# Second-layer linear attention: query products of the second half moved ahead of the key transposes, and the transposes put through four PSUM banks in two rounds

## The chip, the cores and the metric

The kernel runs on one core of one Trainium2 chip. The metric is the time of one execution on the device in microseconds; the time before is 3043.68 us, the median of three runs (3041.82 to 3044.96).

## The reference, cut to what matters

Four images of 64x64 tokens with 128 channels pass through two layers. The first is softmax attention over all 4096 tokens of an image, and takes most of the time. The second has a linear attention, and a routed mixture of experts behind it. The change is in the linear attention:

```python
def _L1_attn_ref(x, W_qkv, W_out, b_out, gn_w, gn_b):
    ...
    qkv = jnp.einsum('oc,bcl->bol', W_qkv, xc)
    q, k, v = jnp.split(qkv, 3, axis=1)
    ...
    q = jax.nn.softmax(q, axis=2) * scale      # over the 32 channels of a head
    k = jax.nn.softmax(k, axis=3)              # over all tokens of an image
    context = jnp.einsum('bhcj,bhdj->bhcd', k, v)
    out = jnp.einsum('bhcd,bhdi->bhci', context, q)
    out = out.reshape(b, h * d, l)
    out = jnp.einsum('oc,bcl->bol', W_out, out) + b_out[None, :, None]
    ...
```

The softmax of the keys runs over all tokens, so the context (a 128x128 matrix) can be summed only once every key chunk has been exponentiated, and no output token exists before the context does.

## The kernel before

The program is written engine by engine, each with its own instruction stream; semaphores tie them together, and each engine works strictly in the order of its stream. The outer loop runs over the four images (batches). Within one, the first layer's attention comes first (512 key tiles of 128 by query chunks of 512), and then the stretch that the change is in, about 75 us of each batch.

In that stretch the 4096 tokens are eight chunks of 512 (`NCH` = 8, `HCH` = 4, `CH` = 512, `TPB` = 4 tiles of 128 a chunk). PSUM has eight banks `BK[0]` to `BK[7]`, one chunk of 512 columns each. Chunk c uses bank c for everything: its transposed input, then its keys (channels by tokens), then its values (tokens by channels), then its queries. Each bank must be read out before TensorE writes it again.

TensorE (`pe`): for each half (chunks 0 to 3, then 4 to 7) it transposes the normed input, makes the keys, then the values. For the first half it makes the queries as well. Then it turns the exponentiated keys K over, chunk by chunk in the order `k_order` = 4, 5, 6, 7, 0, 1, 2, 3, each into its own bank (L1356 to L1364); then makes the queries of chunks 4 to 7 (L1365 to L1367); then sums the context over 32 tiles (L1369 to L1372, into `BK[0]`), which waits for the last copy of the transposed keys. Then the queries, exponentiated and normalised, are turned in the order `q_order` = 1 to 7, 0, and the output products follow.

ScalarE (`act`): copies the first half's values, exponentiates query chunks 0 and 1, exponentiates the keys in two pieces of 2048 columns (L610), copies the second half's values (`values1`, L588), exponentiates query chunks 2 and 3 (L602), copies the eight chunks of transposed keys to `KT` (L617), exponentiates query chunks 4 to 7, and later copies the transposed queries (L621).

VectorE (`dve`): takes each query chunk's maximum over each head (L962), subtracts it and writes `QE` (L963, `q_shifted`), and sums the exponentials and takes the reciprocal (L970, L971, `q_summed`). L988 scales the context to `CTX`, and L993 makes the output weights `AT`. The sums of chunks 5, 6, 7 and 0 stand behind L988 in its stream. GpSimd multiplies `QE` by the reciprocals (L484), chunk by chunk behind L971.

Semaphores at the change: `s_v1c` counts value chunks copied out by ScalarE, `s_q1` query products done, `s_q1s` query chunks read out of PSUM by L963, `s_q1e` query chunks exponentiated, `s_k1e` key exponentials, `s_kT` transposed key chunks in PSUM, `s_kTc` transposed key chunks copied to SBUF.

All matrix work in the trace goes through two helpers: L1134 is any product, L1139 any transpose. A 128x128 product is two MATMUL records, a transpose one.

Of the kernel before, what the change touches and what calls it, by code (L numbers as in the profile page):

```python
# [25 lines left out]
ACT = mybir.ActivationFunctionType  # L26
X_AX = mybir.AxisListType.X

P = 128
B = 4  # L30
N = 64 * 64
C = 128
# [3 lines left out]
CH = 512  # L36
NCH = N // CH
# [74 lines left out]
HCH = NCH // 2  # L112
# [10 lines left out]
def hybrid_kernel(nc, x, w_qkv0, w_out0, b_out0, w_qkvT, w_outT, b_out1, gn_w, gn_b, router_w, router_b,  # L123
# [5 lines left out]
    with ctx:  # L129
        def sb(name, shape, dt=F32, stack=ctx):  # L130
            return stack.enter_context(nc.sbuf_tensor(name, shape, dt))

        def sem(name):
            return ctx.enter_context(nc.semaphore(name))
# [9 lines left out]
        K = sb("K", [P, N])  # L144
# [7 lines left out]
        KT, QE, Z = KE[:, 0:N], KE[:, N:2 * N], KE[:, 2 * N:3 * N]  # L152
# [16 lines left out]
        WQKV1 = sb("WQKV1", [P, 3 * C])  # L169
# [53 lines left out]
        BK = [BK8[:, i, :] for i in range(8)]  # L223
# [60 lines left out]
        s_v1c = sem("s_v1c")  # L284
        s_q1 = sem("s_q1")
        s_q1s = sem("s_q1s")
# [3 lines left out]
        s_kT = sem("s_kT")  # L290
        s_kTc = sem("s_kTc")
# [211 lines left out]
        def _(act):  # L503
            act.sem_inc(s_pvc, 1)
            for b in range(batches):
# [93 lines left out]
                def q_exponentials(chunks):  # L599
                    for c in chunks:  # L600
                        act.wait_ge(s_q1s, b * NCH + c + 1)
                        nc.scalar.activation(QE[:, c * CH:(c + 1) * CH], QE[:, c * CH:(c + 1) * CH],  # L602
                                             ACT.Exp).then_inc(s_q1e, 1)
# [10 lines left out]
                q_exponentials(range(HCH // 2, HCH))  # L614
                for i, c in enumerate(k_order):
                    act.wait_ge(s_kT, b * NCH + i + 1)
                    nc.scalar.activation(KT[:, c * CH:(c + 1) * CH], BK[c], ACT.Copy).then_inc(s_kTc, 1)  # L617
                q_exponentials(range(HCH, NCH))
                for i, c in enumerate(q_order):
                    act.wait_ge(s_qT, b * NCH + i + 1)  # L620
                    nc.scalar.activation(QT[:, c * CH:(c + 1) * CH], BK[c], ACT.Copy).then_inc(s_qTc, 1)  # L621
# [30 lines left out]
        def _(dve):  # L652
# [101 lines left out]
            for b in range(batches):  # L754
# [201 lines left out]
                def q_shifted(chunks):  # L956
                    for c in chunks:
                        g = slice(c * TPB * H, (c + 1) * TPB * H)
                        dve.wait_ge(s_q1, b * NCH + c + 1)
                        q = BK[c].rearrange("p (g d) -> p g d", d=D)  # L960
                        e = QE[:, c * CH:(c + 1) * CH].rearrange("p (g d) -> p g d", d=D)
                        mix_link(v.reduce_max(QM[:, g], q, X_AX))  # L962
                        v.tensor_tensor(e, q, QM[:, g].unsqueeze(2).to_broadcast([P, TPB * H, D]),  # L963
                                        ALU.subtract).then_inc(s_q1s, 1)

                def q_summed(places):
                    for c in q_order[places]:
                        g = slice(c * TPB * H, (c + 1) * TPB * H)
                        dve.wait_ge(s_q1e, b * NCH + c + 1)
                        mix_link(v.reduce_sum(QSUM[:, g], QE[:, c * CH:(c + 1) * CH].rearrange("p (g d) -> p g d", d=D), X_AX))  # L970
                        v.reciprocal(QSUM[:, g], QSUM[:, g]).then_inc(s_q1r, 1)  # L971
# [5 lines left out]
                mix_link(v.reduce_max(SMALL[:, 10:11], MXS[:, :], X_AX))  # L977
                v.tensor_scalar(SMALL[:, 8:9], SMALL[:, 10:11], -1.0, None, ALU.mult).then_inc(s_k1x, 1)
                q_shifted(range(HCH // 2, HCH))
                q_summed(slice(0, HCH - 1))  # L980
                q_shifted(range(HCH, NCH))
                q_summed(slice(HCH - 1, HCH))

                dve.wait_ge(s_k1e, b * 2 + 2)
                mix_link(v.tensor_tensor(SMALL[:, 9:10], KSUM[:, 0:1], KSUM[:, 1:2], ALU.add))
# [146 lines left out]
        def _(pe):  # L1132
            def mm(o, lhsT, rhs, start=True, stop=True, shared=False):
                return nc.tensor.matmul(o, lhsT, rhs, start=start, stop=stop, skip_group_check=shared)  # L1134

            def transposes(dst, src, c):

                for t in range(c * TPB, (c + 1) * TPB):
                    last = nc.tensor.transpose(dst[:, (t % TPB) * P:(t % TPB + 1) * P], src(t), IDENT)  # L1139
                return last  # L1140
# [21 lines left out]
            for b in range(batches):  # L1162
# [169 lines left out]
                def token_major(c, weights, signal):  # L1332
                    for t in range(c * TPB, (c + 1) * TPB):
                        last = mm(BK[c][:, (t % TPB) * C:(t % TPB + 1) * C], XT[:, t * P:(t + 1) * P], weights)
                    last.then_inc(signal, 1)

                for half in range(2):
# [13 lines left out]
                    if half == 0:  # L1351
                        for c in chunks:
                            pe.wait_ge(s_v1c, b * NCH + c + 1)
                            token_major(c, WQKV1[:, 0:C], s_q1)

                for i, c in enumerate(k_order):  # L1356
                    if i % HCH == 0:
                        pe.wait_ge(s_k1e, b * 2 + i // HCH + 1)

                    if c >= HCH:  # L1360
                        pe.wait_ge(s_v1c, b * NCH + c + 1)
                    else:
                        pe.wait_ge(s_q1s, b * NCH + c + 1)
                    transposes(BK[c], lambda t: K[:, t * P:(t + 1) * P], c).then_inc(s_kT, 1)  # L1364
                for c in range(HCH, NCH):  # L1365
                    pe.wait_ge(s_kTc, b * NCH + c - HCH + 1)
                    token_major(c, WQKV1[:, 0:C], s_q1)  # L1367

                pe.wait_ge(s_kTc, b * NCH + NCH)  # L1369
                for t in range(T):  # L1370
# [137 lines left out]
```

## Time and profile before

| | |
|---|---|
| median of three runs | 3043.68 us |
| those runs | 3041.82, 3044.96, 3043.68 us |
| profiled execution, its own time | 3042.56 us |
| its span in the trace | 3040.7 us |
| mean granted TensorE clock | 0.981 of full |
| busy: TensorE, VectorE, ScalarE, GpSimd | 2873.7, 2574.7, 2411.2, 711.9 us |

The span is the time from the first instruction to the last of the profiled execution; 1.9 us of its own time lie around it. In the views, PE is TensorE, PEld its weight loads, DVE VectorE, ACT ScalarE, POOL GpSimd. "L1134" is a line of the kernel.

### The profile page before, as it was taken

The page shows a single profiled execution, that of the slowest core. Times are in us where ns is not written, and L with a number is a line of the kernel's source. Part 1 is how long each engine was busy: PE and PEld are TensorE (multiplying, and loading weights), DVE is VectorE, ACT ScalarE, POOL GpSimd, SP SyncE. Part 2 cuts the span into 40 slices and gives each one's busy share as a digit, 9 for nine tenths or more (in the row PEclk, how much of TensorE's full clock was granted, in tenths as well). Part 3 has the DMA queues.
Part 4 walks back from the last instruction along what each step waited for, and adds up shares of the span by engine and source line. Part 5 has one row for each costly group of instructions (what it writes and reads, how often), then busy time and mean ns, then how long its engine had stood idle before and what let it go on. Part 6 is the DMA issues. An engine that isn't in the chain of part 4 may idle for free.

```text
span 3040.7 us, 52573 instructions
## 1 busy us (share of the span) xinstructions
PE 2873.7 (95%) x20414; PEld 1005.8 (33%) x20414; DVE 2574.7 (85%) x3687; ACT 2411.2 (79%) x3141; POOL 711.9 (23%) x726
## 2 busy tenths in 40 slices
PE   6999999989899999998889999999898999999988
PEld 3222222275422222227532222223743222222474
DVE  5888889878888888887888888898788888888877
ACT  4999999843799999975479999997448999999634
POOL 1122222113412222211432222121153222122115
PEclk9999999998999999999999999999999999999999
DMA  2655565500165555550026555554003555555400
GB/s 86 117 112 106 109 114 113 104 1 14 56 119 107 111 113 109 111 98 1 15 72 117 112 111 111 106 104 92 1 21 61 110 111 112 102 108 109 77 1 28
DMA packets 72081, 257.03 MB, mean 85 GB/s; under 512 B 8160, under 2 KB 10240, under 8 KB 71808
## 3 DMA queue, kind: packets, MB, share of 16 engines
q0 software_dynamic: 64512, 234.91, 40.9%
q1 hardware_dynamic: 7296, 18.51, 1.6%
q8 instruction: 168, 2.75, 0.4%
q14 instruction: 105, 0.86, 0.1%
HBM read 10.12 MB, written 8.39 MB: 6 GB/s over the span
## 4 chain that ended last, share of the span: by engine, by line
PE 84%; DVE 8%; ACT 5%; issue 2%; POOL 1%; SPq 0%; DMA 0%; POOLq 0%; DVEq 0%; ACTq 0%
PE BK L1134 82%; ACT EA L559 2%; DVE X L1103 2%; ACT KE L559 2%; PE BK L1139 2%; DVE MXS L953 1%; DVE ST L679 1%; ACT K L610 1%; POOL KE L484 1%; ACT SMC L548 0%; DVE KE L711 0%; DVE RU L673 0%; DVE RU L672 0%; DVE XT L836 0%; DMA XN<-in_x 0%
## 5 line engine op out<-in xcount | busy, mean ns | idle before, releaser
L889 DVE TENSOR_TENSOR XT<-XT,KE 128x512 f32<-128x512 f32 x1344 | 1573.0, 1227 | 148.9 <-ACT KE L559 146.5
L559 ACT ACTIVATE KE<-BK 128x512 f32<-128x512 f32 (+1 forms) x1536 | 1490.6, 1023 | 129.9 <-PE BK L1134 34.1
L1134 PE MATMUL BK<-Q,K 32*128 32x512 f32 x8192 | 1167.9, 640 | 18.5 <-ACT KE L559 12.2
L1134 PE MATMUL BK<-KE,V 128*32 128x512 f32 x6144 | 815.1, 604 | 5.3 <-ACT SMC L548 5.3
L443 POOL DMA_DIRECT2D RM<-EA x448 | 392.8, 957 | 1506.9 <-ACT EA L559 650.6
L1134 PEld LDWEIGHTS BK<-Q,K 32*128 32x128 f32 x8192 | 320.0, 183 | 874.7 <-ACT KE L559 626.6
L559 ACT ACTIVATE EA<-BK 128x512 f32<-128x512 f32 (+1 forms) x512 | 497.5, 1026 | 26.5
L1134 PEld LDWEIGHTS BK<-KE,V 128*32 128x32 f32 x6144 | 125.4, 108 | 582.7 <-issue 533.0
L1134 PE MATMUL BK<-EA,V 128*32 128x512 f32 x2048 | 272.7, 604 | 0.0
L1134 PE MATMUL BK<-WEXP,XT 128*128 128x512 f32 x512 | 246.0, 628 | 13.9 <-DVE X L1103 13.9
L647 ACT ACTIVATE RM<-BK,GT 128x128 f32<-128x128 f32 x512 | 145.5, 368 | 137.3 <-PE BK L1134 137.3
L1103 DVE SCALAR_TENSOR_TENSOR X<-BK,GT,X 128x128 f32<-128x128 f32 x512 | 175.4, 350 | 33.4 <-PE BK L1134 17.3
L863 DVE TENSOR_TENSOR XT<-KE 128x512 f32<-128x512 f32 x64 | 88.7, 1390 | 124.4 <-ACT KE L559 124.4
L493 POOL TENSOR_TENSOR Z<-RM 128x512 f32<-128x512 f32 x64 | 81.1, 1268 | 266.7 <-ACT RM L647 266.7
L1134 PEld LDWEIGHTS BK<-WEXP,XT 128*128 128x128 f32 x512 | 99.0, 203 | 126.4 <-issue 94.8
L424 POOL TENSOR_TENSOR Q<-PVC,REC 128x512 f32<-128x512 f32 x32 | 70.1, 2192 | 251.0 <-DMA RM<-EA 120.5
L1134 PEld LDWEIGHTS BK<-EA,V 128*32 128x32 f32 x2048 | 40.7, 108 | 193.5 <-issue 171.1
L843 DVE RECIPROCAL REC<-SMC 128x512 f32<-128x512 f32 x28 | 93.7, 3345 | 0.0
L1134 PE MATMUL BK<-WQKV,XT 128*128 128x128 f32 x768 | 89.4, 276 | 0.0
L1134 PEld LDWEIGHTS BK<-WQKV,XT 128*128 128x128 f32 x768 | 87.9, 192 | 4.0 <-issue 3.8
L1134 PE MATMUL BK<-XT,WQKV 128*128 128x512 f32 x192 | 88.1, 613 | 0.5 <-ACT XT L510 0.5
L836 DVE TENSOR_TENSOR XT<-XT,RM 128x512 f32<-128x512 f32 x64 | 75.3, 1217 | 0.0
(182 smaller groups left out, 1803.1 us busy)
## 6 DMA issues: line engine op xcount, KB each, us to landing
RM<-EA POOLq DMA_DIRECT2D x224, 768.0 KB, 6.7
RM<-EA POOLq DMA_DIRECT2D x224, 256.0 KB, 3.3
XN<-in_x SPq DMA_DIRECT2D x16, 512.0 KB, 6.1
out<-X SPq DMA_DIRECT2D x16, 512.0 KB, 2.6
WEXP<-in_L_ffn_expert_w SPq DMA_DIRECT2D x1, 512.0 KB, 6.8
CONST<-in_consts SPq DMA_DIRECT2D x1, 384.0 KB, 5.7
WQKV<-in_L_conv_w_qkv SPq DMA_DIRECT2D x1, 192.0 KB, 2.3
WQKV<-in_L_attn_W_qkv SPq DMA_DIRECT2D x1, 192.0 KB, 5.9
```

Source lines behind the costliest of these rows:

```text
L424: nc.gpsimd.tensor_tensor(Q[:, c * CH:(c + 1) * CH], PVC[:, :], REC[:, :], ALU.mult).then_inc(s_ot, 1)
L443: nc.gpsimd.dma_start(DACC[:, PART[p]], EA[:, k % 2, PART[p]], accum_op=ALU.add).then_inc(s_dacc[p], 16)
L493: nc.gpsimd.tensor_tensor(Z2[:, :, :], z[:, :, 0:2 * C], z[:, :, 2 * C:4 * C], ALU.add).then_inc(s_zs, 1)
L559: nc.scalar.activation(exps(jt, p), scored(c * T + jt, p).rearrange("p a n -> p (a n)"), ACT.Exp, scale=SCALE0).then_inc(s_exp, 1)
L647: last = nc.scalar.activation(ZX[:, t // 2 % 2, t % 2, k], expert_bank(t, 1)[:, k], ACT.Copy, scale=GT[:, t, e:e + 1])
L836: v.tensor_tensor(acc, acc, DACC[:, PART[p]], ALU.add).then_inc(s_merge, 1)
L843: v.reciprocal(REC[:, :], row_sums).then_inc(s_rec, 1)
L863: v.tensor_tensor(ACC[:, par, PART[p]], exps(0, p), exps(2, p), ALU.add).then_inc(s_adds, 1)
L889: v.tensor_tensor(acc, acc, exps(jt, p), ALU.add).then_inc(s_adds, 1)
L1103: v.scalar_tensor_tensor(X[:, t, :], expert_bank(t, 0)[:, e * C:(e + 1) * C], GT[:, t, e:e + 1], X[:, t, :], ALU.mult, ALU.add).then_inc(s ...
L1134: return nc.tensor.matmul(o, lhsT, rhs, start=start, stop=stop, skip_group_check=shared)
L1139: last = nc.tensor.transpose(dst[:, (t % TPB) * P:(t % TPB + 1) * P], src(t), IDENT)
```

## The change

TensorE makes the second half's queries before any key transpose. The transposes then take banks 0 to 3 only, the place in the order taken modulo four: the first four (chunks 4 to 7) wait until VectorE has read the first half's queries from those banks, the last four (chunks 0 to 3) until ScalarE has copied out the transposed chunk that was put there one round earlier. ScalarE's four query exponentials of the second half, which came behind the eight copies, are put between them, one behind every second copy. VectorE sums one query chunk instead of three before it takes the second half's queries, and three instead of one behind them. No instruction is added or left out.

```diff
@@ ScalarE
                 for i, c in enumerate(k_order):
                     act.wait_ge(s_kT, b * NCH + i + 1)
-                    nc.scalar.activation(KT[:, c * CH:(c + 1) * CH], BK[c], ACT.Copy).then_inc(s_kTc, 1)
-                q_exponentials(range(HCH, NCH))
+                    nc.scalar.activation(KT[:, c * CH:(c + 1) * CH], BK[i % HCH], ACT.Copy).then_inc(s_kTc, 1)
+                    if i % 2:
+                        q_exponentials([HCH + i // 2])
@@ VectorE
                 q_shifted(range(HCH // 2, HCH))
-                q_summed(slice(0, HCH - 1))
+                q_summed(slice(0, 1))
                 q_shifted(range(HCH, NCH))
-                q_summed(slice(HCH - 1, HCH))
+                q_summed(slice(1, HCH))
@@ TensorE
+                for c in range(HCH, NCH):
+                    pe.wait_ge(s_v1c, b * NCH + c + 1)
+                    token_major(c, WQKV1[:, 0:C], s_q1)
                 for i, c in enumerate(k_order):
                     if i % HCH == 0:
                         pe.wait_ge(s_k1e, b * 2 + i // HCH + 1)
 
-                    if c >= HCH:
-                        pe.wait_ge(s_v1c, b * NCH + c + 1)
+                    if i < HCH:
+                        pe.wait_ge(s_q1s, b * NCH + i + 1)
                     else:
-                        pe.wait_ge(s_q1s, b * NCH + c + 1)
-                    transposes(BK[c], lambda t: K[:, t * P:(t + 1) * P], c).then_inc(s_kT, 1)
-                for c in range(HCH, NCH):
-                    pe.wait_ge(s_kTc, b * NCH + c - HCH + 1)
-                    token_major(c, WQKV1[:, 0:C], s_q1)
+                        pe.wait_ge(s_kTc, b * NCH + i - HCH + 1)
+                    transposes(BK[i % HCH], lambda t: K[:, t * P:(t + 1) * P], c).then_inc(s_kT, 1)
```

## Rows read from the trace of the kernel before

**Rows 1.** The page: busy time by engine, and the chain's shares.
```profile
PE 2873.7 (95%) x20414; PEld 1005.8 (33%) x20414; DVE 2574.7 (85%) x3687; ACT 2411.2 (79%) x3141; POOL 711.9 (23%) x726
...
PE 84%; DVE 8%; ACT 5%; issue 2%; POOL 1%; SPq 0%; DMA 0%; POOLq 0%; DVEq 0%; ACTq 0%
```

**Rows 2.** Windows, batches 1 and 2: length, busy PE, PEld, DVE, ACT, POOL, clock, DMA.
```profile
610.00:800.00 190.00, 168.48 (x830) 118.22 (x829) 150.24 (x450) 91.63 (x239) 53.12 (x57) 0.91 0.03 12
1361.00:1551.00 190.00, 166.41 (x850) 114.89 (x851) 153.06 (x460) 91.42 (x241) 53.14 (x57) 0.94 0.03 12
```

**Rows 3.** The chain that ended last, fourth batch: start us, us, what.
```profile
2899.38 0.49 ACT V L588
...
2915.99 0.35 DVE CTX L988
...
2917.30 4.08 POOL KE L484 x4
...
2922.14 7.16 PE BK L1134 x64
```

**Rows 4.** TensorE's timeline there: start us, us, line, operation, [idle before, releaser].
```profile
2892.73 3.73 PE L1134 MATMUL BK<-WQKV,XT 128*128 128x128 f32 x32
2900.00 5.15 PE L1139 MATMUL BK<-CONST,K 128*128 128x128 f32 x32 [3.54 <-ACT V L588]
2904.99 3.74 PE L1134 MATMUL BK<-WQKV,XT 128*128 128x128 f32 x32
2908.56 7.31 PE L1134 MATMUL BK<-V,KE 128*128 128x128 f32 x64
2915.71 1.91 PE L1139 MATMUL BK<-CONST,KE 128*128 128x128 f32 x16
```

**Rows 5.** ScalarE's timeline there.
```profile
2899.28 2.03 ACT L588 ACTIVATE V<-BK 128x512 f32<-128x512 f32 x4
2901.19 1.16 ACT L602 ACTIVATE KE<-KE 128x512 f32<-128x512 f32 x2
2902.23 4.01 ACT L617 ACTIVATE KE<-BK 128x512 f32<-128x512 f32 x8
...
2902.23 0.60 ACT L617 ACTIVATE KE<-BK 128x512 f32<-128x512 f32 x1
...
2916.35 2.07 ACT L621 ACTIVATE EA<-BK 128x512 f32<-128x512 f32 x4 [4.21 <-PE BK L1139]
```

**Rows 6.** VectorE's timeline there.
```profile
2897.83 0.67 DVE L970 TENSOR_REDUCE QSUM<-KE 128x16 f32<-128x512 f32 x1
2898.53 0.25 DVE L971 RECIPROCAL QSUM<-QSUM 128x16 f32<-128x16 f32 x1
...
2906.09 0.69 DVE L962 TENSOR_REDUCE QM<-BK 128x16 f32<-128x512 f32 x1 [2.41 <-PE BK L1134]
...
2907.42 0.68 DVE L962 TENSOR_REDUCE QM<-BK 128x16 f32<-128x512 f32 x1
```

**Rows 7.** Short windows, columns as in rows 2.
```profile
644.40:650.00 5.60, 5.55 (x26) 5.58 (x27) 1.74 (x4) 5.10 (x11) 2.05 (x2) 0.50 0.01 3
...
2900.00:2903.00 3.00, 3.00 (x14) 3.00 (x15) 1.10 (x3) 3.00 (x7) 0.08 (x1) 0.50 0.00 0
2903.10:2904.90 1.80, 1.80 (x19) 1.80 (x18) 0.54 (x2) 1.80 (x5) 1.80 (x2) 1.00 0.00 0
...
1493.20:1496.60 3.40, 3.40 (x8) 1.84 (x9) 2.31 (x5) 0.00 (x0) 0.00 (x0) 0.52 0.00 0
...
677.50:680.80 3.30, 3.30 (x6) 1.75 (x7) 2.26 (x14) 0.00 (x0) 0.00 (x0) 0.51 0.01 2
```

**Rows 8.** TensorE's timeline at three other pauses, batches 1 and 2.
```profile
1493.14 1.00 PE L1436 MATMUL BK<-CONST,G 128*128 128x128 f32 x4 [2.63 <-DVE GT L1084]
```
```profile
1476.62 1.98 PE L1134 MATMUL BK<-WEXP,XT 128*128 128x512 f32 x4 [1.59 <-DVE X L1103]
```
```profile
676.40 0.38 PE L1134 MATMUL BK<-MV,CONST 128*128 128x1 f32 x2 [1.31 <-DVE MV L1002]
```

## The prediction, as it was made before the result was known

> **What bounds the kernel now.** The page says that TensorE is busy 95% of the span and carries 84% of the chain that ended last [rows 1], but that is an average in which the first layer weighs most. The change touches only the second layer's linear attention, so I read the chain of waits there, in the fourth batch [rows 3]. The reader is to see that no engine has slack in it. ScalarE's first value copy, on the chain from 2899.38 behind the key exponentials, frees a bank, TensorE starts at 2900.00 and works without a pause through the key transposes (32 records), the query products (32) and the context (64), until 2915.87 [rows 4]; then VectorE scales the context, GpSimd normalises four query chunks and TensorE makes the output. Whatever moves the start of the context moves the end of the batch by the same amount, unless something behind it was waiting for another engine. The other batches have the same chain with the same pieces, so each cost counts four times.
>
> TensorE's timeline [rows 4] gives the four numbers to hold on to: a pause of 3.54 us up to 2900.00, the queries' products from 2904.99, the context from 2908.56, its end at 2915.87. ScalarE's timeline [rows 5] shows why that context starts without a wait: the eight copies of transposed keys run from 2902.23 to 2906.24, while TensorE transposes and then makes queries. The last copy ends 2.3 us before the context needs it. **The query products are what hides the copies.** The change takes that cover away.
>
> **What starts TensorE.** Before, the first transpose waits for the copy of the values in bank 4 (s_v1c). After, the first query product waits for the same copy, since queries of chunk 4 go to bank 4. So TensorE starts again at 2900.0, and the pause of 3.54 us stays. Banks 0 to 3 would have been free earlier, but the transposes that use them stand behind the products. Gain at the start: nothing, from either side; only a reordering of the stream could give one.
>
> **TensorE's 64 records.** The stretch from 2900.0 begins at half clock (1.2 GHz, granted 0.50) and is at full clock (2.4 GHz) from about 2903.0 [rows 7]. At full clock 32 product records run in 3.57 us (2904.99 to 2908.56 [rows 4]), 0.112 us each, and the 16 transposes of rows 4 in (1.91 - 0.28)/15 = 0.109 us each. Product and transpose records cost the same, so it does not matter which of them fall into the slow 3 us: 32 transposes now take 4.99 us there (2900.00 to 2904.99), and 32 products will too. Products end at 2905.0, transposes follow. Sum so far: 0.
>
> **VectorE.** A chunk has 8 product records: 1.8 us at half clock for chunk 4. VectorE starts a chunk 1.10 us after its product starts at full clock (2904.99 to 2906.09 [rows 4, 6]), so 0.2 us after its records; chunk 4 can be taken from 2902.0. Each chunk costs 1.33 us (2906.09 to 2907.42 [rows 6]), so the shifted queries are there at about 2903.4, 2904.7, 2906.0 and 2907.4. Only one sum (L970 and L971, some 0.9 us from 2897.83 [rows 6]) stands ahead of them now. Then three sums of some 0.9 us, to 2910.1, all before the context's scaling. The sums of chunks 5, 6, 7 and 0 still stand behind L988, so the tail from the context to the output (rows 3: 2915.99 to 2922.14, with GpSimd's 4.08 us) is not shortened. Gain: 0.
>
> **ScalarE, and the term that decides.** Spacing of copies: (4.01 - 0.60)/7 = 0.487 us, where 0.60 is one copy [rows 5]. Spacing of exponentials: 2901.19 to 2902.23 for two, 0.52 each [rows 5]. A transposed chunk is 4 records, 0.44 us, and ScalarE starts 0.64 us after its first record (2915.71 to 2916.35 [rows 4, 5]). So:
>
> - the first transpose starts at 2905.05, the first copy at 2905.69;
> - transposes come every 0.44 us and copies every 0.487, so from there ScalarE has a queue and never waits;
> - before the eighth copy it does seven copies and three exponentials: 7 x 0.487 + 3 x 0.52 = 4.97 us, and the exponentials' inputs (2903.4 to 2906.0) are always there in time. The eighth copy starts at 2910.66 and ends at 2911.26;
> - TensorE follows 0.13 us behind a copy's end (2899.38 + 0.49, transpose at 2900.00 [rows 3, 4]). The context starts at 2911.39 instead of 2908.56: **2.83 us later**.
>
> TensorE itself hardly waits for banks: its fifth transpose is ready at 2906.8, the first copy done at 2906.3; the seventh waits about 0.2 us, the eighth 0.3. It has turned the last chunk by 2909.1, and then stands idle for some 2.3 us. That is where the loss shows. Four batches: 4 x 2.83 = 11.3 us. The fourth exponential falls behind the last copy and costs nothing.
>
> Bounds of this term. If the exponentials cost nothing between the copies, 4.97 shrinks to 3.41, and the context starts 1.27 us late: 5.1 us in all. If every step of ScalarE took its full 0.60 us instead of overlapping the next, ten steps would be 6.0 us and the delay 3.86: 15.4 us in all. I take the measured spacings, since copies and exponentials already stand next to each other without a gap: values to 2901.19, two exponentials, then copies from 2902.23 [rows 5].
>
> **The clock.** The new pause is on TensorE's path, and the clock may fall behind it. Rows: the pause of 2.63 us ahead of L1436 is followed by 3.4 us at half clock (granted 0.52), in all four batches alike; a pause of 1.59 us by none; one of 1.31 us with a small product and 0.7 us more, 2 us in all, by half clock in the first batch only, 3.3 us at 0.51 [rows 7, 8]. Mine is 2.3 us plus two short waits, nearer to 2.63. A stretch of 3.4 us at half clock costs 1.7 us, some of it spent in the pause itself; 1.5 us then. I take three batches of four: 4.5 us. Bounds: nothing, and 4 x 1.7 = 6.8 us. Beside this, shifting the later batches changes where other slow stretches fall: batch 1 now has a mean of 0.91 over 190 us, batch 2 0.94 [rows 2], which is 0.03 x 190 = 5.7 us of full clock between two batches with the same work. That can go either way, and widens the range on both sides, more upward, because three of the four batches show the better figure now (0.94, 0.94, and the fourth the same stretches).
>
> By the Trainium skill, page "TensorE: Matmul & The Clock Gate", section "Part 4: PE-mode transpose", transposes do not count as activity for the clock, so that products placed first should bring it back sooner. In this trace the clock came back at 2903.0 behind 3 us of transposes alone, so I give this no term; by the rule, 3 us at half clock would shrink at most to 0 and return 1.5 us a batch.
>
> **Sum.** Own time of the profiled execution 3042.56 + 11.3 + 4.5 = 3058.4 us; against the median, 3043.68, that execution is 1.1 us short. I forecast 3058.4 us.
>
> **Rivals.**
>
> A. ScalarE's queue as above, but the clock stays up in the new pause, or nearly: 3042.56 + 11.3 = 3053.9. For it: 1.59 us left the clock alone. Against it: 2.63 us never did. Chance 0.20.
>
> B. Only latency: the copies keep pace with the transposes because the exponentials cost almost nothing there, and only the last copy is bare: 3042.56 + 5.1 = 3047.7, with at most a clock fall or two. Against it stands 0.52 us each. Chance 0.08, part of it within 0.2% (6.1 us), which is about what a measurement of this kernel can tell from no change.
>
> C. The other side, not slower: the clock. Its place is the start at 2900.0 and the slow stretches behind it. In the first batch the half clock lasts from before 644.4 to beyond 650.0, 26 records, where the others have 3 us from the restart [rows 7]. If products first, or the shifted phase, brought the clock back earlier, a batch would win up to 1.5 us at 2900 (2.8 in the first) and up to 5.7 us over the rest of the first batch. It decides only from 11.3 us on, that is, 22.6 us less at half clock in all; 1.5 x 3 + 2.8 + 5.7 = 13.0 would do it, if all of it came and the new pause cost nothing. Chance 0.03. The Trainium skill, in the section on transposes named above ("TensorE: Matmul & The Clock Gate", Part 4), would speak for the first part of it, 1.5 us a batch.
>
> D. No effect: the products would have to go on hiding the copies, or the tail have slack of 2.8 us. GpSimd's and VectorE's pieces behind the context are bare in the chain, so I see none. Chance 0.03.
>
> E. Worse: all four pauses drop the clock, and the shifted batches pick up more slow stretches: 3053.9 + 6.8 = 3060.7, and up to 5.7 more, 3066.4. Chance 0.16.
>
> My forecast (queue and two to four falls of the clock, 3056 to 3061) has 0.50. To hold eight in ten the range runs from 3051 to 3065: it leaves out B, C, D and the end of E. Faster by over 0.2%: 0.02; within 0.2% (up to 3049.8): 0.07; slower: 0.91.
>
> **What the profile of the changed kernel would show.** The start of the query products, 3.5 us behind the values, as before: right for the first step. The last key transpose some 2 us ahead of the context, with the context's idle put down to ScalarE's L617: right for the queue. Spacing of 0.49 and 0.52 us on ScalarE from the first copy to the eighth: right for its price; gaps there would mean that VectorE or TensorE sets the pace. The distance from the context's end to the output's start unchanged at 6.3 us. Granted clock 0.5 behind the pause in most batches. I am wrong if the context starts less than 1.5 us later than before relative to the first value copy, or if the tail behind it shortens.

## The result, and the profile after

The changed kernel takes 3057.32 us (median of five runs, 3055.97 to 3059.27), against 3043.04 us for the kernel before (five runs). The ratio is 1.0047, 95% interval 1.0036 to 1.0057: slower by 14.3 us, between 11 and 17. The prediction was 3058.4 us, range 3051 to 3065. The profiled execution took 3055.97 us, span 3054.2 us, 13.5 us more span than before.

In the changed kernel lines behind 979 stand one further down: products are L1135, transposes L1140, the scaling of the context L989. First the chain that ended last in the fourth batch (start us, us, what), to be laid beside [rows 3]:

```profile
2910.64 5.18 PE BK L1135 x32
2915.82 0.45 PE BK L1140 x4
...
2916.29 1.09 ACT KE L617 x2
2917.38 0.52 ACT KE L602
2917.90 0.97 ACT KE L617 x2
2918.87 0.52 ACT KE L602
2919.39 0.97 ACT KE L617 x2
2920.36 0.52 ACT KE L602
2920.88 0.98 ACT KE L617 x2
...
2921.91 7.43 PE BK L1135 x64
...
2929.43 0.35 DVE CTX L989
```

Before, the chain stayed on TensorE from 2900.00 to the context's end:

```profile
2900.00 5.15 PE BK L1139 x32
2905.15 10.73 PE BK L1134 x96
```

Now it leaves TensorE behind the first transposed chunk, runs over eleven steps of ScalarE (eight copies, three exponentials), and comes back only for the context. TensorE's timeline of the same stretch, beside [rows 4]:

```profile
2910.64 5.18 PE L1135 MATMUL BK<-WQKV,XT 128*128 128x128 f32 x32 [3.44 <-ACT V L588]
2915.66 3.92 PE L1140 MATMUL BK<-CONST,K 128*128 128x128 f32 x32
2921.91 7.41 PE L1135 MATMUL BK<-V,KE 128*128 128x128 f32 x64 [2.32 <-ACT KE L617]
```

In this batch the restart is as before (a pause of 3.44 us, then 32 records in 5.0 us), the transposes follow, and ahead of the context stands a new pause of 2.32 us, released by the copy. All four batches have it, at 2.32 or 2.33 us.

The distances, taken from TensorE's timelines (start of the first record of each kind, us). "Restart" is the first record behind the pause of 3.5 us, "output" the first output product, "the next attention" the next batch's first product of queries and keys:

| batch | restart to context, before | after | context to output, before | after | output to the next attention, before | after |
|---|---|---|---|---|---|---|
| first | 9.91 | 12.77 | 13.42 | 15.15 | 143.52 | 141.60 |
| second | 8.44 | 11.51 | 13.42 | 13.52 | 141.60 | 141.59 |
| third | 8.53 | 11.55 | 13.42 | 13.51 | 141.62 | 142.98 |
| fourth | 8.56 | 11.27 | 13.42 | 13.52 | 118.72 (to the end) | 118.77 |

The context is late by 2.86, 3.07, 3.02 and 2.71 us, 11.7 in all. From there to the output only the first batch differs much: 1.73 us. The rest of the batch gives 1.9 back in the first and takes 1.4 more in the third. Sum: 11.7 + 2.0 - 0.5 = 13.2, and some 0.3 us ahead of the restarts make the 13.5 of the spans.

The 11.7 us have two parts, by the same timelines. From the first key transpose to the context it is 6.25 us in every batch, where it was 3.57 from the first query product to the context: 2.68 us a batch, 10.7 in all. The other 0.95 us lie in the 32 records behind the restart. As query products they take 6.52, 5.26, 5.30 and 5.02 us, where the 32 transposes before took 6.33, 4.87, 4.96 and 4.99.

The clock behind the new pause, in windows (length, busy PE, PEld, DVE, ACT, POOL, then the granted clock), first and second batch:

```profile
657.20:661.00 3.80, 3.77 (x19) 3.77 (x20) 0.00 (x0) 0.49 (x1) 0.00 (x0) 0.55 0.00 0
...
1413.00:1416.00 3.00, 3.00 (x27) 3.00 (x28) 0.00 (x0) 0.42 (x1) 0.19 (x1) 1.00 0.00 0
```

The reader is to see the same pause and two outcomes: half clock behind it in the first batch, full clock in the second. The third and fourth are like the second.

### The profile page after: what moved, and what is told of

The parts are those of the page before. It is cut to its first block, busy times and chain, and to the rows that moved or that the text cites. A ratio compares the mean times of both kernels' runs of the same rounds, so it can differ in the third digit from the quotient of the medians.

```text
span 3054.2 us, 52573 instructions
## 1 busy us (share of the span) xinstructions
PE 2881.0 (94%) x20414; PEld 1014.4 (33%) x20414; DVE 2576.3 (84%) x3687; ACT 2410.4 (79%) x3141; POOL 710.9 (23%) x726
## 4 chain that ended last, share of the span: by engine, by line
PE 83%; DVE 8%; ACT 6%; issue 2%; POOL 1%; DMA 0%; SPq 0%; POOLq 0%; DVEq 0%; ACTq 0%
PE BK L1135 82%; ACT EA L559 2%; DVE X L1104 2%; ACT KE L559 2%; PE BK L1140 1%; DVE MXS L954 1%; DVE ST L680 1%; ACT K L610 1%; POOL KE L484 1%; ACT KE L617 1%; ACT SMC L548 0%; DVE KE L712 0%; DVE RU L674 0%; DVE RU L673 0%; DVE XT L837 0%
## 5 line engine op out<-in xcount | busy, mean ns | idle before, releaser
L1135 PE MATMUL BK<-Q,K 32*128 32x512 f32 x8192 | 1167.8, 640 | 18.5 <-ACT KE L559 12.2
L1135 PE MATMUL BK<-KE,V 128*32 128x512 f32 x6144 | 815.0, 604 | 5.3 <-ACT SMC L548 5.3
L1135 PEld LDWEIGHTS BK<-Q,K 32*128 32x128 f32 x8192 | 319.9, 182 | 874.8 <-ACT KE L559 626.6
L1135 PEld LDWEIGHTS BK<-KE,V 128*32 128x32 f32 x6144 | 125.3, 108 | 582.7 <-issue 533.0
L1135 PE MATMUL BK<-EA,V 128*32 128x512 f32 x2048 | 272.6, 604 | 0.0
L1135 PE MATMUL BK<-WEXP,XT 128*128 128x512 f32 x512 | 239.1, 613 | 13.9 <-DVE X L1104 13.9
L1135 PEld LDWEIGHTS BK<-WEXP,XT 128*128 128x128 f32 x512 | 95.6, 196 | 122.3 <-issue 90.3
L1135 PE MATMUL BK<-WQKV,XT 128*128 128x128 f32 x768 | 97.2, 290 | 13.8 <-ACT V L588 13.8
L1135 PEld LDWEIGHTS BK<-EA,V 128*32 128x32 f32 x2048 | 40.7, 108 | 193.5 <-issue 171.1
L1135 PEld LDWEIGHTS BK<-WQKV,XT 128*128 128x128 f32 x768 | 95.3, 205 | 18.5 <-ACT V L588 14.5
L1135 PE MATMUL BK<-XT,WQKV 128*128 128x512 f32 x192 | 89.0, 618 | 0.5 <-ACT XT L510 0.5
```

## The experiments

Each was timed against the kernel before on the same chip. A figure such as "+14" is us over it. None of the kernels leaves work out; the added transposes of four of them (e4, e5, e8, e9) write into a bank that is overwritten before anything reads it. A row with fewer than 64 records of V,KE is cut off by the end of the view, not by the kernel.

### e1: the exponentials back behind the copies

```diff
                     nc.scalar.activation(KT[:, c * CH:(c + 1) * CH], BK[i % HCH], ACT.Copy).then_inc(s_kTc, 1)
-                    if i % 2:
-                        q_exponentials([HCH + i // 2])
+                q_exponentials(range(HCH, NCH))
```

> The changed kernel with ScalarE's four exponentials of the second half put back behind the eight copies; TensorE and VectorE as changed. Theory (ScalarE's queue decides when the context starts): before the eighth copy there are seven copies and no exponential, 3.41 instead of 4.97 us, so from the first query product to the context it is about 9.8 us in a batch, against 8.5 before and 11.3 to 11.6 in the changed kernel; the time is some 5 us over before, with the clock up to 8. Rival (the loss comes from the clock, or from products ahead of transposes as such): the distance stays at 11 us or more and the time at 13 to 14 us over before.

Measured: 3043.03 us against 3043.37, ratio 0.9998 (0.9989 to 1.0007). The mechanism came as worked out and the total did not. TensorE's timeline, second batch:

```profile
1398.48 5.44 PE L1134 MATMUL BK<-WQKV,XT 128*128 128x128 f32 x32 [3.44 <-ACT V L588]
1403.76 3.66 PE L1139 MATMUL BK<-CONST,K 128*128 128x128 f32 x32
1408.48 3.73 PE L1134 MATMUL BK<-V,KE 128*128 128x128 f32 x31 [1.06 <-ACT KE L617]
```

The pause has shrunk from 2.33 to 1.06 us, and restart to context is 10.00 us (fourth batch 9.93): 1.5 us less than in the changed kernel in the second batch, and 1.4 to 1.6 more than before. From the first key transpose to the context it is 4.72 us in every batch, where it was 6.25: the three exponentials cost 1.53 us in the queue, and 1.56 were worked out for them. Yet those 1.4 us, four times, are nowhere in the total. They are won back behind the output in all four batches: output to the next attention takes 140.14 and 140.17 us in the second and third batch, where it took 141.60 and 141.62. My theory of the queue stands; that delays simply add up does not. e8 asks why. e1 also divides the loss: the products moved ahead of the transposes, with the four banks, cost nothing in the total, and the 14 us come only with the exponentials put between the copies. The exponentials there, with the products left behind the transposes, were not run.

### e2: the sums in their old order

```diff
                 q_shifted(range(HCH // 2, HCH))
-                q_summed(slice(0, 1))
+                q_summed(slice(0, HCH - 1))
                 q_shifted(range(HCH, NCH))
-                q_summed(slice(1, HCH))
+                q_summed(slice(HCH - 1, HCH))
```

> The changed kernel with VectorE's sums in their old order (three chunks ahead of the second half's queries, one behind). Theory: VectorE takes chunk 4's queries about 1.5 us later, and they are still there before ScalarE asks for them behind its second copy; nothing moves, 14 us over before as the changed kernel. Rival (VectorE's order is what holds ScalarE): ScalarE waits at its exponentials and the time rises by a further 2 us or more.

Measured: 3057.68 us, ratio 1.0044 (1.0028 to 1.0059), +14, as the changed kernel. Restart to context is 11.55 us in the second batch (after: 11.51), and ScalarE's steps stand as close as before. VectorE's new order does nothing.

### e3: the four banks alone

TensorE, ScalarE and VectorE in their old orders, and only the banks of the transposes changed, with the waits that this asks for (ScalarE's copy, not shown, reads the same bank):

```diff
                 for i, c in enumerate(k_order):
                     if i % HCH == 0:
                         pe.wait_ge(s_k1e, b * 2 + i // HCH + 1)
-                    if c >= HCH:
-                        pe.wait_ge(s_v1c, b * NCH + c + 1)
+                    if i < HCH:
+                        pe.wait_ge(s_q1s, b * NCH + i + 1)
                     else:
-                        pe.wait_ge(s_q1s, b * NCH + c + 1)
-                    transposes(BK[c], lambda t: K[:, t * P:(t + 1) * P], c).then_inc(s_kT, 1)
+                        pe.wait_ge(s_kTc, b * NCH + i - HCH + 1)
+                    transposes(BK[i % HCH], lambda t: K[:, t * P:(t + 1) * P], c).then_inc(s_kT, 1)
                 for c in range(HCH, NCH):
-                    pe.wait_ge(s_kTc, b * NCH + c - HCH + 1)
+                    pe.wait_ge(s_v1c, b * NCH + c + 1)
                     token_major(c, WQKV1[:, 0:C], s_q1)
```

> The old order on TensorE (transposes, then products of the second half) and old orders on ScalarE and VectorE, but the transposes through four banks in two rounds. Theory (what was lost is the cover of the products over the copies): the first round runs inside the old pause, some 2 us earlier, the second waits for the copies and ends at about the time at which it ended before; products cover the last copies again, so the context starts within 0.5 us of before and the time is within 3 us of before. Rival (the two rounds in four banks cost in themselves): 5 us or more over before.

Measured: 3041.58 us against 3043.37, ratio 0.9992 (0.9983 to 1.0001). No loss.

```profile
1394.37 1.97 PE L1139 MATMUL BK<-CONST,K 128*128 128x128 f32 x16 [0.99 <-ACT K L610]
1399.91 3.41 PE L1139 MATMUL BK<-CONST,K 128*128 128x128 f32 x16 [3.57 <-ACT KE L617]
1403.11 3.97 PE L1134 MATMUL BK<-WQKV,XT 128*128 128x128 f32 x32
1406.92 3.29 PE L1134 MATMUL BK<-V,KE 128*128 128x128 f32 x28
```

The first round runs in what was the pause, because banks 0 to 3 are free early; the second waits 3.57 us for ScalarE's first key copy, and then runs at half clock (3.41 us for 16 records that took 1.97 in the first round). The products cover the last copies, as I expected: the context follows them without a wait. But it does not start within 0.5 us of before. Counted from the start of the key exponentials on ScalarE (1392.22 here), it is 14.70 us, where it was 13.14 before in that batch (1393.69 to 1406.83): 1.6 us late, and in the first batch 0.1. So e3 is a second kernel, after e1, that is late by some 1.5 us in most batches and not slower. Its output to the next attention is 140.2 us in the second batch, like e1's. What it settles is that the two rounds in four banks do not cost time in themselves.

### e4: the old pause filled

```diff
+                pe.wait_ge(s_q1s, b * NCH + 1)
+                for _ in range(7):
+                    transposes(BK[0], lambda t: XT[:, t * P:(t + 1) * P], 0)
                 for i, c in enumerate(k_order):
```

> The kernel before, with 28 extra transposes into bank 0 in TensorE's 3.5 us pause ahead of the key transposes; what they write is overwritten. It prices the clock alone. Theory: the clock stays at full behind the pause, and the distance from the first key transpose to the context falls from 8.5 us (9.9 in the first batch) to 7.1; 1.4 us in three batches and 2.8 in the first, so 7 us less than before. Rival (transposes do not keep the clock up, or the clock is set by something else): no difference, or a later restart, 0 to 2 us more.

Measured: 3039.89 us, ratio 0.9987 (0.9978 to 0.9996), -3.5.

```profile
1392.40 3.22 PE L1139 MATMUL BK<-CONST,XT 128*128 128x128 f32 x28
1396.11 3.77 PE L1139 MATMUL BK<-CONST,K 128*128 128x128 f32 x32 [0.48 <-ACT V L588]
1399.71 3.74 PE L1134 MATMUL BK<-WQKV,XT 128*128 128x128 f32 x32
1403.29 1.95 PE L1134 MATMUL BK<-V,KE 128*128 128x128 f32 x16
```

Restart to context is 7.18 us in every batch: 1.3 to 1.4 less in three, 2.7 in the first, 6.7 in all, as expected. The transposes in the pause hold the clock up. But about half of it is lost later: output to the next attention takes 142.0 us in the first batch and 143.7 and 142.1 in the next two, where it took 143.5, 141.6 and 141.6, and in the fourth it is 120.7 us from the output to the end, where it was 118.7. That is 3.0 us back, net.

### e5: the new pause filled

```diff
+                pe.wait_ge(s_q1s, b * NCH + HCH + 1)
+                for _ in range(5):
+                    transposes(BK[4], lambda t: K[:, t * P:(t + 1) * P], 0)
                 pe.wait_ge(s_kTc, b * NCH + NCH)
```

> The changed kernel with 20 extra transposes into bank 4 behind the key transposes, in the new pause of 2.3 us; what they write is overwritten. Theory (the pause costs its length, through ScalarE's queue, and only now and then the clock): the context starts as late as in the changed kernel; the clock falls behind it in no batch, which is worth 1.6 us where it fell (one batch in the profile of the changed kernel); the time is 12 to 14 us over before. Rival (most of the loss is the clock's): the time comes back to 5 to 8 us over before.

Measured: 3053.85 us against 3042.51, ratio 1.0037 (1.0024 to 1.0049), +11.3, just below what I had written. In the first batch the context starts 12.69 us behind the restart, as late as after (12.77), but the output follows 13.52 us later instead of 15.15. That is the 1.6 us of the clock; the other batches are nearly unchanged from restart to output (11.36 and 11.46 us to the context in the second and third). The new pause costs its length. Its clock costs some 3 of the 14 us by the medians (the two intervals overlap), and 1.6 in the profiles from restart to output.

### e8 and e9: the kernel before, with a delay alone

```diff
                 pe.wait_ge(s_kTc, b * NCH + NCH)
+                for _ in range(3):      # six in e9
+                    transposes(BK[1], lambda t: XT[:, t * P:(t + 1) * P], 0)
```

> The kernel before, with 12 extra transposes into bank 1 between the last key copy and the context, in every batch; what they write is overwritten. At full clock they take 12 x 0.11 = 1.3 us, so the context starts about as late as with the exponentials put back behind the copies (1.4 us a batch later than before), and that kernel was not slower than before. Theory (a delay of this size moves the slow stretches of TensorE's clock behind it, and what the batch loses ahead of the output it wins back there): within 2 us of before. Rival (delays simply add up, and that kernel won its time in another way): 5 us over before.

> The same with 24 extra transposes, 2.6 us, so the context starts nearly as late as in the changed kernel (2.7 to 3.1 us a batch later than before), with no other part of the change. Theory (the changed kernel's loss is the late context, four times, and what the clock makes of it): 10 to 14 us over before. Rival (the change costs in another place as well): at most 8 us over before.

Measured: e8 3044.50 us against 3042.79, ratio 1.0005 (0.9996 to 1.0014), +1.7. e9 3054.49 us, ratio 1.0042 (1.0028 to 1.0055), +11.7. In the second batch the context is 9.88 and 11.22 us behind the restart: 1.4 and 2.8 late. 1.4 us in each batch cost next to nothing in all, 2.5 to 2.8 us cost 11.7. Here is where e8 wins back, in windows of the second batch: the routing products and transposes, and the pause ahead of the second gates (before, then e8, then after):

```profile
1443.80:1470.00 26.20, 23.75 (x119) 17.61 (x118) 21.31 (x81) 6.74 (x22) 2.71 (x3) 0.80 0.00 1
1490.00:1500.00 10.00, 7.37 (x17) 3.44 (x16) 7.98 (x22) 3.25 (x12) 3.32 (x5) 0.83 0.00 0
```
```profile
1445.60:1471.30 25.70, 23.75 (x119) 17.64 (x118) 21.04 (x81) 6.69 (x21) 2.72 (x3) 0.80 0.00 1
1491.30:1501.30 10.00, 7.37 (x27) 3.72 (x26) 8.69 (x24) 4.16 (x15) 4.84 (x6) 1.00 0.01 2
```
```profile
1450.00:1476.20 26.20, 24.91 (x109) 19.46 (x108) 19.80 (x77) 6.09 (x18) 1.99 (x2) 0.67 0.00 1
1496.20:1506.20 10.00, 7.37 (x24) 3.50 (x23) 8.69 (x25) 4.03 (x16) 4.15 (x5) 1.00 0.00 0
```

Each has the same pause of 2.63 us ahead of the gates' transposes [rows 8]. In the kernel before the clock falls behind it (0.83 over 10 us, 17 matmul records in it); in e8 it does not (1.00, 27 records), and neither does it in the changed kernel, which pays in the routing stretch instead (0.67 where the others have 0.80, and 109 records in 26.2 us where before has 119: the window is as long, but the work in it is less). Over the same work, from the first routing product (WR) to the first run of twelve expert products (WEXP), it is 25.9 us before, 25.7 in e8 and 27.6 after; from the gates' transposes to the next attention 68.7, 67.0 and 67.0. Over output to the next attention, e8 takes 140.17 us in the second batch, before and after 141.6. So a delay ahead decides which of several slow stretches fall where. e8 confirms that a pure delay of 1.4 us is compensated for the greater part, without any other part of e1. Why the clock falls behind one pause of 2.63 us and not behind another is not settled by these runs.

The timelines of all kernels, laid side by side, show more than e8 alone. This is the length of a batch, from the start of one context to the start of the next (us; e6 and e7 are described below):

| kernels | second context to third | third to fourth |
|---|---|---|
| before, e1, e3, e8 | 750.83, 750.98, 751.05, 750.91 | 750.90, 750.95, 750.99, 751.12 |
| e4 | 751.53 | 750.57 |
| after, e2, e5, e9 | 754.25, 754.30, 754.23, 754.54 | 754.71, 754.71, 754.24, 754.04 |
| e6 | 747.70 | 747.61 |
| e7 | 744.05 | 744.23 |

The lengths lie in four groups with nothing between them. Contexts that are 1.2 to 1.6 us late leave the batch within 0.3 us of its length before; contexts that are 2.5 to 3.1 us late make it longer by 3.1 to 3.8 us, more than the delay. Each kernel was profiled once, and the interval from the first context to the second does not fall into the same groups (752.47 us before, 755.72 after), but the medians of all executions lie in the same order. Why the lengths come in groups is open.

It bears on e9, too. Its profile is 12.0 us longer than that of the kernel before, as much as four late contexts (10.7 us), but not by four equal parts: 2.3 us stand already ahead of the first restart (646.77 us, before 644.45), where the two kernels are the same; the first late context (12.49 us behind the restart, before 9.91) is won back in the rest of its batch; and the later ones cost more than their lateness. That four delays of some 2.7 us and a loss of 11.7 us agree so nearly is in part chance.

### e6: the first round in the old pause, products between

```diff
+                for i in range(HCH):
+                    key_turned(i)
+                second_query(HCH)
+                second_query(HCH + 1)
+                for i in range(HCH, NCH):
+                    key_turned(i)
+                second_query(HCH + 2)
+                second_query(HCH + 3)
@@ ScalarE, in place of values1, q_exponentials and the loop of copies
+                values1(HCH)
+                values1(HCH + 1)
+                for i in range(HCH):
+                    key_copied(i)
+                values1(HCH + 2)
+                values1(HCH + 3)
+                for i in range(HCH, NCH):
+                    key_copied(i)
+                q_exponentials(range(HCH // 2, NCH))
```

`key_turned`, `second_query` and `key_copied` are the bodies of the loops of the changed kernel, with its waits.

> The first round of key transposes stands first and runs inside the old pause (banks 0 to 3 are free 2 us before bank 4 is); then query products of chunks 4 and 5, the second round, products of chunks 6 and 7, the context. ScalarE copies values 4 and 5, keys of round one, values 6 and 7, keys of round two, and exponentiates query chunks 2 to 7 behind them. Theory: ScalarE's twelve copies from 2899.3 take 12 x 0.48 = 5.8 us, so the last one ends at 2905.2, and TensorE's 48 records left take 5.3 us from 2900.4 at full clock; the context starts at 2905.7 to 2907 instead of 2908.56, 1.5 to 2.8 us earlier a batch, 6 to 11 us less than before. Rival (the start of the context isn't set by copies and cover but by TensorE's records and clock alone): within 2 us of before.

Measured: 3025.91 us against 3042.51, ratio 0.9946 (0.9933 to 0.9960), -16.6, more than expected.

```profile
2883.24 1.97 PE L1146 MATMUL BK<-CONST,K 128*128 128x128 f32 x16 [0.99 <-ACT K L610]
2885.71 2.05 PE L1141 MATMUL BK<-WQKV,XT 128*128 128x128 f32 x16 [0.50 <-ACT V L588]
2887.60 1.91 PE L1146 MATMUL BK<-CONST,K 128*128 128x128 f32 x16
2889.34 1.95 PE L1141 MATMUL BK<-WQKV,XT 128*128 128x128 f32 x16
2891.13 7.35 PE L1141 MATMUL BK<-V,KE 128*128 128x128 f32 x64
```

The pause of 3.54 us has become one of 0.99 and one of 0.50, the clock stays up, and the context starts 10.0 us behind the key exponentials' start (2881.09) where it was 13.3 before (2895.30 to 2908.56) and 15.9 after (2906.02 to 2921.91). That is 3.1 to 3.2 us in the last three batches and 4.6 in the first (14.61 before, 10.04 here), 14.1 in all, where 6 to 11 was expected. The upper estimate of 2.8 us a batch already had the 48 records at full clock (5.3 us; they take 5.42); its miss of 0.4 us is mostly the restart, 4.62 us behind the key exponentials' start, where I had counted 5.1. What it left out is the first batch, whose slow stretch was longer: 1.4 us more. The remaining 2.5 us are not assigned; the batches from the second context on are 3.1 and 3.3 us shorter than before (the table above).

### e7: e6, and all sums ahead of the context's scaling

```diff
-                q_summed(slice(1, HCH))
+                q_summed(slice(1, NCH))
                 dve.wait_ge(s_k1e, b * 2 + 2)
                 ...
-                q_summed(slice(HCH, NCH))
                 dve.wait_ge(s_ctx, b * 2 + 2)
```

> As the kernel with the first round in the pause, and VectorE's last four sums ahead of the context's scaling, so that GpSimd normalises while the context is summed. Theory (the tail from the context to the output is set by GpSimd's 4.08 us behind those sums): exponentials end at 2908.3, sums at about 2912, GpSimd at about 2914, near the context's end; the tail shrinks from 6.3 us to about 4, another 2 us a batch, 14 to 19 us less than before in all. Rival (VectorE's sums end behind the context and only change places): no gain over the kernel without it.

Measured: 3015.45 us against 3042.51, ratio 0.9904 (0.9889 to 0.9920), -27 us, where 14 to 19 less was expected. It beats both kernels. It gains 10.5 us over e6, where some 8 were expected; the rest of the surplus is e6's own. GpSimd's timeline, then TensorE's, fourth batch:

```profile
2889.48 7.09 POOL L484 TENSOR_TENSOR KE<-KE,QSUM 128x512 f32<-128x512 f32 x7 [8.42 <-DVE QSUM L978]
```
```profile
2886.47 7.34 PE L1140 MATMUL BK<-V,KE 128*128 128x128 f32 x64
2893.65 1.91 PE L1145 MATMUL BK<-CONST,KE 128*128 128x128 f32 x16
2895.40 0.39 PE L1140 MATMUL BK<-WOUT,CTX 128*128 128x128 f32 x2
2895.62 1.91 PE L1145 MATMUL BK<-CONST,KE 128*128 128x128 f32 x16
2897.37 7.31 PE L1140 MATMUL BK<-AT,EA 128*128 128x128 f32 x64
```

GpSimd works while the context is summed, and the second four query transposes no longer wait for it. Context to output is 10.9 us where it was 13.4: 2.5 us a batch.

## Why the prediction was right

**The restart** was to gain nothing, and the pause 3.5 us to stay. It is 3.44 us. Right.

**TensorE's records**: 32 products in the slow stretch in 5.0 us, as many as the transposes before; measured 5.02 (2910.64 to 2915.66) in the fourth batch. Right there, and too small elsewhere: in the other three the products take 0.19, 0.39 and 0.34 us more than the transposes did, 0.95 us in all with the fourth's 0.03, for which the prediction had 0.

**VectorE**: no part in it. Right, and e2 shows it: the old order of the sums gives the same time and the same distance.

**ScalarE's queue**, the term that decides: 2.83 us a batch, 11.3 in all, was forecast; the contexts are late by 2.86, 3.07, 3.02 and 2.71, 11.7. The agreement within 0.4 us is of two misses with opposite signs: the queue itself is 2.68 us a batch, 10.7 in all, and the rest is the products' 0.95. About half of the 0.15 us by which the queue was priced too high is its last step: TensorE follows the last copy within 0.05 us (2921.86 to 2921.91), where I had taken 0.13. The chain after shows its steps as I had priced them, 0.97 for two copies and 0.52 for an exponential, a pause of 2.32 us (forecast 2.3). e1 takes the exponentials out and the distance falls by 1.5 us, against 1.56. The tail from the context's end to the output is unchanged, as forecast; read from TensorE's timeline it is 6.1 us in both kernels, not 6.3.

**The clock** was mis-sized. I had said that it falls behind the new pause in three batches of four, 4.5 us. It fell in one of four in the profiled execution, and cost 1.6 us there; e5, which fills the pause, is 11.3 us over before where the changed kernel is 14.3. I had argued from the pause of 2.63 us, behind which the clock fell in all four batches of the kernel before. In three of the changed kernel's four batches, and in e8's second to fourth, the same pause, of the same length, is followed by full clock. Its four repetitions were nearly one observation made four times, since the later batches repeat the timing of the one ahead (750.83 and 750.90 us from context to context). The 2.9 us by which this term was too large in the profile (13.4 measured there, 15.8 forecast, with 0.4 us from the late contexts the other way) is nearly the whole miss. The profiled execution is the shortest of the five; against the medians, which differ by 14.3 us, the sum is 1.5 us too large.

**Adding up.** The prediction said that whatever moves the start of the context moves the end of the batch by the same amount, and so counted the queue four times. For this change the total agrees with that, in part by luck. e1 and e8 show that it need not be so: contexts late by 1.2 to 1.6 us a batch cost nothing in e1 and 1.7 us in e8, where 5 to 6 would be the sum; e3 is a third case. By the table behind e9 a batch did not grow by its delay, but by next to nothing or by more than 3 us, and a delay of 2.7 to 3.1 us lies near the second. Had the change carried only its first half, without the interleaved exponentials, I would have forecast 5 us slower, and e1, which is that half, is no slower. So the price of the late context is shown; that it counts in full, and four times, was taken for granted, and the runs bear it out only for delays of this size.

**The rivals.** A (the clock stays up, 3053.9) described the profile of three batches of four well; the profiled execution, 3055.97, lies between A and the forecast, a little nearer to A, and the median, 3057.32, is nearer to the forecast. B is excluded by the 0.52 us steps in the chain. C: the clock did not come back sooner with products first, some 3 us at 0.50 as before in the fourth batch (e1 and after both need 5.0 to 5.3 us for 32 products, outside the first batch). Its other half, that the shifted phase gives time back, is what e1 and e8 show at a lateness of 1.4 us. D is excluded by the chain. E: the third batch picked up 1.4 us, no more.

## What to carry to other kernels

Before moving work ahead on one engine, ask what it was hiding: here products of 3.6 us stood between eight transposes and the sum that needs their copies, and the new order put nothing else there. Price the engine that drains, step by step, with whatever is queued between the steps, from the first input to the last copy; that gave the queue's 10.7 us within 0.6. Then test whether a delay reaches the total at all: here 1.4 us a batch did not. And look at both ends of the path for the waits themselves: splitting the transposes so that one half fills the pause and the other sits between products, and taking four sums out from behind the context, gave 27 us, where moving the cover alone cost nothing and moving it with three exponentials in the queue lost 14.

## What the runs showed of the hardware that was not expected

In this kernel, where TensorE's clock changes level often, delays in a repeated stretch did not add: 1.4 us a batch cost 1.7 us over four batches, 2.5 to 2.8 us a batch cost 11.7 (e8, e9). The length of a batch, from the second context on, lay near 744.1, 747.6, 751.0 or 754.4 us in eleven kernels and never between. The windows show that which later stretches run at half clock changes along with the delay; that this is the whole cause is not shown.

The same pause of 2.63 us was followed by half clock in one kernel (before, second batch: 0.83 over 10 us) and by full clock in another (e8: 1.00), in which the same instructions stand around it and come 1.6 us later.

Filling a pause with transposes kept the clock at full in all four batches (e4: 7.18 us for what took 8.4 to 9.9), and about half of the gain was lost again downstream.
